# A two-layer transformer block on one core: order of the sums of squares, and one gelu read straight from PSUM

## The reference, cut to what matters

```python
qkv = shift_token(x) @ wqkv              # 8 heads of 64
q, k = l2norm(q) * qs, l2norm(k) * ksc   # norm of each head's 64 numbers
q, k = rotary_xpos(q, k)                 # q*cos*scale + rotate_half(q)*sin*scale
o = local_attention(q, k, v)             # windows of 64 tokens, own and previous one
x = x + o @ wo
h = layernorm(shift_token(x)) @ w1 + b1  # 2 * 341 columns
a, g = split(h)
x = x + (a * gelu(g)) @ w2 + b2
```

## Time and profile before

| what | value |
|---|---|
| median of 3 runs | 1572.35 (1572.09 to 1573.59) |
| the profiled execution | 1571.71 |
| its span | 1569.9 |
| busy over the span: PE, DVE, ACT, POOL | 92%, 83%, 78%, 57% |
| granted clock of PE, mean | 0.978 |
| 700 to 800 us: PE, DVE, ACT, POOL busy, of 100 | 98.3, 89.4, 84.2, 69.2 |

### The profile page before, as it was taken

How to read it: one execution, slowest core, us unless ns; L and a number is a source line. 1 busy time by engine, 2 the same in 40 slices (tenths; PEclk the granted TensorE clock), 3 DMA queues, 4 the chain that set the end, 5 groups by cost and what they waited for, 6 DMA issues and landing times.

```text
span 1569.9 us, 46462 instructions
## 1 busy us (share of the span) xinstructions
PE 1445.2 (92%) x18975; PEld 1121.2 (71%) x18975; DVE 1300.5 (83%) x1692; ACT 1231.8 (78%) x1834; POOL 897.2 (57%) x626
## 2 busy tenths in 40 slices
PE   5999997889999999999998767989999999999998
PEld 3777874777777777777776554777777777777776
DVE  6777757888899999898885866988998998988884
ACT  4876867788888888888885857788888888888884
POOL 4334104666666666766761645776666666667761
PEclk9999999999999999999999878999999999999999
DMA  4312003675566756656650003666666565565562
GB/s 115 111 51 91 11 7 70 132 128 117 119 122 126 115 118 127 122 123 120 120 105 20 0 8 71 134 132 111 122 127 120 117 123 122 124 119 123 113 110 67
DMA packets 359855, 157.46 MB, mean 100 GB/s; under 512 B 299410, under 2 KB 335836, under 8 KB 359644
## 3 DMA queue, kind: packets, MB, share of 16 engines
q1 hardware_dynamic: 359644, 154.51, 49.0%
HBM read 27.29 MB, written 6.29 MB: 21 GB/s over the span
## 4 chain that ended last, share of the span: by engine, by line
PE 54%; ACT 20%; DVE 11%; issue 5%; DMA 4%; SPq 4%; POOL 1%; DVEq 0%; POOLq 0%; ACTq 0%
PE PS L199 8%; PE PS L201 7%; PE PS L200 7%; PE PS L852 6%; DMA t<-t 4%; PE PS L827 4%; PE PS L871 4%; ACT t L1059 3%; PE PS L834 3%; PE PS L860 3%; ACT t L1143 2%; PE PS L914 2%; DVE t L1256 2%; ACT L1200 2%; ACT L1143 2%
## 5 line engine op out<-in xcount | busy, mean ns | idle before, releaser
L1432 POOL TENSOR_TENSOR t<-t 128x1024 f32<-128x1024 f32 x128 | 308.2, 2408 | 207.8 <-DVE t L1262 207.4
L1438 POOL TENSOR_TENSOR t<-t 128x512 f32<-128x512 f32 x256 | 320.5, 1274 | 150.5 <-DVE t L1272 150.2
L1272 DVE TENSOR_TENSOR t<-t 128x1024 f32<-128x1024 f32 x128 | 208.5, 1629 | 0.1
L199 PE MATMUL PS<-wqh,HH 128*128 128x512 f32 x384 | 179.8, 468 | 21.0 <-DVE t L1262 10.9
L1256 DVE TENSOR_REDUCE t<-t 128x16 f32<-128x1024 f32 x128 | 156.0, 1219 | 33.3 <-ACT t L1059 32.2
L1291 DVE TENSOR_REDUCE t<-PS 128x8 bf16<-128x1024 f32 x128 | 156.1, 1220 | 16.9 <-PE PS L801 16.7
L1279 DVE TENSOR_TENSOR t<-t,PS 128x1024 bf16<-128x1024 f32 x128 | 155.1, 1212 | 9.9 <-ACT PS L1079 9.6
L1079 ACT CAST PS<-t 128x1024 f32<-128x1024 bf16 x128 | 130.2, 1017 | 41.6 <-DVE t L1291 32.2
L852 PE MATMUL PS<-t 128*64 128x65 f32 x4096 | 147.5, 224 | 13.0 <-DVE t L1325 13.0
L1262 DVE SCALAR_TENSOR_TENSOR t<-t,PS 128x1024 f32<-128x1024 f32 x128 | 155.0, 1211 | 0.6 <-ACT t L1066 0.6
L201 PE MATMUL PS<-wqh,HL 128*128 128x512 f32 x384 | 152.8, 398 | 0.0
(11 more groups left out here) (242 smaller groups left out, 3411.9 us busy)
## 6 DMA issues: line engine op xcount, KB each, us to landing
t<-t SPq DMA_DIRECT2D x254, 130.0 KB, 2.4
t<-turns SPq DMA_DIRECT2D x128, 128.0 KB, 2.8
t<-yT SPq DMA_DIRECT2D x108, 128.0 KB, 2.4
t<-t SPq DMA_TRANSPOSE x304, 3.4
t<-in_c_rope SPq DMA_DIRECT2D x32, 128.0 KB, 2.2
turns<-t SPq DMA_DIRECT2D x32, 128.0 KB, 1.9
t<-in_L_attn_a_x SPq DMA_DIRECT2D x4, 512.0 KB, 7.0
t<-yT SPq DMA_DIRECT2D x16, 127.8 KB, 2.6
```

The costliest lines, as they stand in the source:

```text
L199: e.matmul(o, ah, bh, start=not more, stop=False, skip_group_check=True)
L1272: e.e.tensor_tensor(BL.ta[i % 2].rearrange("p (x h) d -> p x h d", x=2), BL.qn.rearrange("p (x h) d -> p x h d", x=2), cos.to_broadcast([1 ...
L1432: e.e.tensor_tensor(BL.tc.rearrange("p (x h) d -> p x h d", x=2), BL.qn.rearrange("p (x h) d -> p x h d", x=2), sin.to_broadcast([128, 2, ...
L1438: e.e.tensor_tensor(tv[:, :, 32 * s:32 * s + 32], tv[:, :, 32 * s:32 * s + 32], BL.tc[:, :, 32 * (1 - s):32 * (1 - s) + 32], ALU.add).then ...
```

## The change

Three things are changed, in both passes.

1. ACT: `squares(s)` stands in front of `copy_result(s-4)`, in all steps but those where `chunk_at(s, 13)` is a chunk (the step after a gelu step), which keep the order.
2. ACT, gelu step: `gate` of part 2 is gone. `gelu_there(C, 2, 6)`, which existed for the last chunks, reads bank 6 with its bias, applies gelu and writes SBUF; it stands behind `rnorms` and ahead of the other two gelus. PE's wait for bank 6 before `gather` in that step is now for this gelu. The counts of two semaphores follow, and `gated` waits for all three gelus.
3. DVE, gelu step: `norms(s)` stands in front of `rope(s-1)`. `normed` has a further wait, for `rope` of the tile before.

```diff
-            return (3 * NC - 4) * u + 3 * C + i + 1
+            return 2 * (NC - 1) * u + 2 * C + i + 1
...
                 if chunk_at(s, 12) is not None:
-                    e.wait_ge(S.ff_ev, evicted(u, chunk_at(s, 12), 2))
+                    e.wait_ge(S.ff_ge, 3 * (NP * u + chunk_at(s, 12)) + 1)
...
+                behind_gelus = chunk_at(s, 13) is not None
+                if on(0) and not behind_gelus:
+                    squares(s)
                 if on(4):
                     copy_result(s - 4)
...
-                if on(0):
+                if on(0) and behind_gelus:
                     squares(s)
                 if s == 0:
                     norm(range(7, 8))
-                if chunk_at(s, 12) is not None:
-                    gate(chunk_at(s, 12), 2, 6)
...
                 if chunk_at(s, 12) is not None:
-                    gelus(chunk_at(s, 12), range(3))
+                    gelu_there(chunk_at(s, 12), 2, 6)
+                    gelus(chunk_at(s, 12), range(2))
...
                 e.wait_ge(S.la_tc, hi(i - 1) + 1)
+                e.wait_ge(S.la_ta, hi(i - 1) + 1)
...
                 e.wait_ge(S.ff_l, n + 1)
-                e.wait_ge(S.ff_ge, n + 1)
+                e.wait_ge(S.ff_ge, n + 1 if C >= NC - 2 else n - i + 3)
...
+                if on(0) and chunk_at(s, 12) is not None:
+                    norms(s)
                 if on(1):
                     rope(s - 1)
...
-                if on(0):
+                if on(0) and chunk_at(s, 12) is None:
                     norms(s)
```

## The result

The changed kernel takes 1557.79 (median of 4 runs, 1554.74 to 1560.03), the kernel before 1572.97 (4 runs, 1572.09 to 1576.93): ratio 0.9897, 95% interval 0.9873 to 0.9922, 15.2 us faster. Forecast were 1561.3 and a range of 1555 to 1570, which holds the measured median; the forecast's narrower range of 1558 to 1565 misses it by 0.2.

A forecast was written before the change was run, and what follows sets the result against it. PE sets the pace, so only its waits can be won. Terms 10.7 - 3.2 + 3.8 - 1.5 + 1.2 = 11.0 off 1571.71 give 1560.7, median 1561.3; range 1555 to 1570.

The forecast's parts named there:

- `gather` two steps after the gelus: PE's `gather` two steps after a gelu step starts 0.41 earlier, 26 times: 10.7 us gained.
- later copy, gelu step and three after: PE's bank-7 product loses 0.06 to the later copy in 28 + 26 places: 3.2 us lost.
- later copy, first steps of a pass: Before the first chunk, the later copy exposes `project_out` by up to 0.49; taken as zero, upper bound 8.8.
- step after the gelus, chunks 1 to 7: PE's 0.43 stall of `values` goes; the full 0.43 left in 8 of 14 periods, nothing in 5: 3.8 us gained.
- the same, chunks 8 to 12: POOL's later adds slow DVE's next cosine product to about 2.4; the step loses 0.15 in 10 periods: 1.5 us.
- first gelu step: First gelu step of each pass, where `values` waits 1.9: `exps` come about 0.6 earlier, 1.2 us for both passes.
- The rival with the copy exposed all through: Slower: the copy, 0.49 later in 80 steps, is fully exposed, costing 39, time 1597; chance 0.08.
- Bank 6: Gelu step: bank 6 is free 0.8 before `gather` needs it; without norms ahead, late by some 0.1.
- only the first gain holds: `gated` of part 1 or transposes bind all 24 periods one step after the gelus: 5.1 gained, 1567.3; chance 0.15.
- the change moves idle time only: PE waits at the transposes or at DVE for what it no longer waits for here: time 1572; chance 0.11.
- The port costs nothing: Chunks 8 to 12 win 0.27 on average instead of losing, time 1557.1; chance 0.1.
- The drain behind the table load: Gelu step: a 1.4 delay behind the table load makes `gather` 0.6 late in 26 steps, time 1577; chance 0.04.

The follow-up runs named there:

- Norms behind the cosine again: Changed kernel with norms behind the cosine's product again; squares ahead and the third gelu from its bank stay: 1555.67 (one run).
- the changed kernel with the residual later: Changed kernel, but POOL adds second-layer chunks' residual two steps after the gelus, not in the gelu step: 1553.86 (5 runs), ratio 0.9884; again 1556.89, 0.9906.

## Why the prediction came out, point by point

Direction and size were right: 11.0 forecast, 11.7 between the two profiled executions, 14.0 in the loops. The medians differ by 15.2, since the changed kernel's profiled execution stood 2.2 above its median and that of the kernel before 1.3 below its own. The terms, as differences of the means over the two passes, which add up to the 14.0:

| term | forecast | measured |
|---|---|---|
| `gather` two steps after the gelus | 26 x 0.41 = 10.7 | 8.3 (26 x 0.31 = 8.1 where nothing else holds the step) |
| later copy, gelu step and three after | -3.2 | -0.7 (0.07 a period where nothing else holds it) |
| later copy, first steps of a pass | 0 | -1.3 (steps 3 to 11) |
| step after the gelus, chunks 1 to 7 | 3.8 | 14 x 0.35 = 4.9 |
| the same, chunks 8 to 12 | -1.5 | -1.4 |
| first gelu step (without its share of the first row) | 1.2 | 4.2, of which 3.0 are two falls of the clock |

That 11.7 stands so near 11.0 is partly luck: the first row is 2.4 too large, the copy's two rows together 1.2 too severe, and the last row lacks 3.0 for a fall of PE's clock, which the prediction does not have at all. The stretch outside the loops, 2.3 longer in the profile after, took the surplus off again.

- *Two steps after the gelus.* "DVE is free for it, since `norms` comes earlier too" was wrong by 0.1. I read the step from a period in which PE had just waited 0.38 for a transpose, and DVE had used that time. In the other periods the cosine product ends later against `project`, and `norms` and `scaled` queue behind it. Transposes then take some of it in the first layer (the mean is 0.21 there), and in the second the step wins 0.48, of which 0.17 is what the step before had lost.
- *Step after the gelus.* The size was right, the cause was not. `exps` come 0.68 earlier and the stall of 0.43 goes, 9.16 to 8.73, in ten of the 14 periods (I had eight), and transposes take some back in four. But I gave the gain to norms ahead of the cosine. Squares alone make 0.34 of it; norms in front add 0.08 in a period without a transpose's wait, and in the second layer they bring the loss. The experiment without squares shows the order of norms as a loss by itself: a wait for work that is still late, with the cosine product queued behind. The term came out since I had costed the edits together.
- *Later copy.* Costed at 0.06 a place, 0.12 a period; (c) and (d) together are 0.07 longer in a period without another wait. In the means 0.7 is left, since the kernel before had two waits for transposes in these steps that the profile after does not have. The rival with the copy exposed all through is out.
- *Bank 6.* The cover was there, 0.8 in the rows, but it did not hang on the order of norms.
- *Second layer.* Confirmed to 0.01 per period, and by moving the residual. What I missed is that the following step wins it back.
- *First gelu step.* I took 0.6 per pass and it was 2.1. The windows show why (rows as explained under "Norms behind the cosine again"). They go from the same product (L903) to the `gather` of the step, over the same 34 matmuls. Before, in the first pass:

```profile
354.10:358.29 4.19, 4.19 (x34) 2.81 (x32) 1.97 (x2) 2.86 (x6) 1.57 (x2) 0.59 0.54 109
```

and the changed kernel:

```profile
355.25:357.91 2.66, 2.66 (x34) 1.87 (x32) 2.24 (x3) 2.21 (x6) 2.34 (x2) 1.00 0.66 124
```

Before, PE stood still for 1.9 in one piece, and then ran most of this window at the lower clock (1.2 GHz, half of full): mean 0.59, and the same work took 1.5 longer. In the second pass it stood still for 2.7 and the clock fell too. Now PE waits 1.26 at `gather` and 0.3 at `values`, and the clock stays at 1.00:

```profile
348.59 1.15 PE L852 MATMUL PS<-t 128*64 128x65 f32 x32 [1.26 <-ACT t L1150]
```

What decides is not shown. With the three parts together, with or without the third gelu from its bank, the clock stayed at 1.00 there in all 16 passes profiled; PE's longest single wait was 1.24 to 1.84. With squares alone it fell in one pass of four (waits of 2.07 to 2.38; steps 11 to 13 take 20.4 with the fall and 18.9 without), and with the order of before in three of four (1.92 to 2.72; the pass with 2.70 was without a fall). Without norms ahead, or without squares ahead, it fell in four of four (2.12 to 2.60). This points to a worth of norms ahead in this first step, 1.5 for each fall that does not come, though one kernel with and without the fall shows that chance has a part. The 1.2 that is left of the term is what I forecast. The Trainium skill, page "TensorE: Matmul & The Clock Gate", Part 1, says that TensorE's clock is gated by how busy the engine has recently been; the falls behind a wait and none in the busy stretches from step 16 to step 64 agree with it.

- *The first steps of a pass.* I took zero since PE waited for transposes behind the copy. That holds in the first pass and not in the second, where the steps take 1.1 to 1.8 longer (65.6 and 66.3 in two profiles of the changed kernel, 64.5 before). The bound of 8.8 was far off.

Of the rivals, "only the first gain holds" and "the change moves idle time only" are refuted by (a) and the loops. "The port costs nothing" is refuted by the 2.44 and 1.67, though its time of 1557.1 is the nearest to the measured median: its number came out for another reason. The drain behind the table load is refuted by the gelu that starts 0.01 after it.

Partly open: why steps 3 to 11 of the first pass take 71 with the old order behind the changed kernel's later steps, in two profiles of two, and 66.4 to 68.6 in the others. A fall of the clock makes about 1.5 of it, behind a wait for a transpose of 2.6 and 2.8; the 68.6 has such a fall too, the profiles from 66.4 to 67.9 have none. Why that transpose came so late is not shown.

## What to carry to other kernels

On an engine with several releasers, put first what can start first, if the one behind has slack; here a swap of two ScalarE instructions won 1% alone. To move a consumer forward before its producer is early costs time, 12 us here: it turns a free wait into one that the queue stands behind. Once the producer was early, the move added 0.08 a period in one layer and nothing in the sum until the residual was out of its way. Read a step's slack from a period without an odd wait, and cost parts of a change one by one too, since a right sum may hide a wrong cause.

## What the runs showed of the hardware

The part of the span that no edit touched took 468.2 to 475.7 in 14 profiles. Most of it lies before the first pass: from the first exp of the self-attention (39.6 to 41.6) to the first gather of the pass it is 226.6 to 231.7. The granted clock divides the profiles in two. In nine of them it falls to half twice in that stretch, near 120 and near 233, and they took 230.8 to 231.7; in the other five it does not fall from 43 us on until the stretch's last 12 us, and they took 226.6 to 228.1. The kernel before, and the changed kernel with the residual later:

```profile
110.00:130.00 20.00, 18.22 (x72) 14.42 (x72) 16.99 (x21) 14.51 (x20) 13.25 (x8) 0.91 0.17 52
225.00:245.00 20.00, 14.50 (x45) 8.63 (x44) 8.96 (x18) 11.15 (x19) 3.84 (x3) 0.91 0.16 42
```

```profile
110.00:130.00 20.00, 17.33 (x75) 13.55 (x73) 18.25 (x25) 13.24 (x19) 12.78 (x9) 1.00 0.19 59
225.00:245.00 20.00, 14.84 (x44) 7.37 (x43) 11.06 (x20) 14.69 (x27) 3.84 (x3) 1.00 0.21 52
```

The two kernels have the same instructions there, so this goes with the execution and not with the edit. It hides an effect of 3 us that the loops show clearly, and the best single time of all, 1549.12 with the residual later, is from one of the five. What makes an execution fall in one group or the other is not shown.

A DVE product with two SBUF inputs that starts behind a POOL product takes its own 1.22 when POOL has ended, and 1.67, 2.44 or 3.23 when it starts 1.8, 1.05 or 0.24 behind the start of POOL's. In each of the last three cases it ended 1.08 to 1.09 after POOL's did. In the rows above, 711.72 + 2.41 + 1.08 = 715.21 = 712.77 + 2.44. Twice in the kernel before DVE's started 0.04 ahead of POOL's: then DVE's took its 1.22 and POOL's 3.4 for 2.4. The profile shows such a wait as a longer instruction and not as idle time.
